# Moving small steps between the scans of a fused state-space and expert kernel, and one more pair of C products a chunk onto VectorE

## The reference

```
xn = LN(x)
B_t = xn @ W_B.T ; C_t = xn @ W_C.T                  # 16 numbers a row each
dt  = softplus((xn @ W_dt1.T) @ W_dt2.T + b_dt2)     # 256 a row
A   = -exp(log_A)                                    # 256 x 16
h   = exp(dt*A) * h + ((exp(dt*A) - 1)/A) * xn * B_t # for each of 256 x 16, along time
y   = sum over the 16 of h * C_t ; x1 = x + y + D_skip * xn
x2  = x1 + expert(LN(x1))                            # the expert of 8 with the largest logit,
                                                     # gelu(v @ W1 + b1) @ W2 + b2, 1024 hidden
```

## Time and profile before

| | |
|---|---|
| runs | 818.1 us median of 3 (811.09, 818.1, 821.95) |
| profiled execution | 813.52 us, of it 811.5 us span |
| busy in the span | TensorE 705.9 (87%), VectorE 526.8 (65%), ScalarE 480.7 (59%), GpSimd 513.6 (63%) |
| scans | from 34.0 to 489.2 us, eight chunks of 54.3 to 64.4 us |
| experts and end | from there to 811.5 us |

### The profile page before, as it was taken

The page is one execution under the profiler, slowest core; times in us unless marked ns, Lnnn a source line. Parts: engine busy times, 40 slices in busy tenths (PEclk is TensorE's granted clock), DMA queues, the critical chain, the costliest instruction groups (busy, mean ns, idle before and its releaser), DMA issues. The chain is left out here.

```text
span 811.5 us, 17757 instructions
## 1 busy us (share of the span) xinstructions
PE 705.9 (87%) x5882; PEld 614.9 (76%) x5883; DVE 526.8 (65%) x903; ACT 480.7 (59%) x983; POOL 513.6 (63%) x643
## 2 busy tenths in 40 slices
PE   7589798798898997986996877969999999999993
PEld 6467687677676776875776766759999999999992
DVE  4769988889988889888789986344333343333430
ACT  3388888888898997878875765313223332233320
POOL 1499987888879877989987775533333433334320
PEclk9579989899999998998987898789999999999997
DMA  9766853342343343464535459331111111111000
GB/s 211 178 215 215 276 175 94 103 133 67 108 141 105 90 122 98 85 108 102 96 92 57 110 174 310 47 41 46 57 44 59 36 42 48 47 54 46 29 8 1
DMA packets 45768, 82.61 MB, mean 102 GB/s; under 512 B 7800, under 2 KB 16253, under 8 KB 45696
## 3 DMA queue, kind: packets, MB, share of 16 engines
q1 hardware_dynamic: 39680, 69.08, 32.0%
q0 software_dynamic: 6016, 12.61, 6.0%
HBM read 70.50 MB, written 13.91 MB: 104 GB/s over the span
## 5 line engine op out<-in xcount | busy, mean ns | idle before, releaser
L628 POOL TENSOR_TENSOR w_sb<-w_sb,Csb 128x512 f32<-128x512 f32 x218 | 275.0, 1274 | 60.8 <-DVE w_sb L1178 42.6
L1178 DVE TENSOR_TENSOR_SCAN w_sb<-WW,hlast,w_sb 128x512 f32<-128x512 f32 x164 | 201.3, 1267 | 15.0 <-PE WW L994 12.0
L858 ACT ACTIVATE dt<-WW,b1c 128x128 f32<-128x128 f32 x312 | 89.2, 368 | 201.4 <-PE WW L1076 201.4
L979 PEld LDWEIGHTS WW<-b_sb,xin 64*128 64x128 f32 x2048 | 136.3, 202 | 73.4 <-issue 35.1
L979 PE MATMUL WW<-b_sb,xin 64*128 64x130 f32 (+1 forms) x2048 | 162.0, 301 | 34.3 <-DVE w_sb L1178 22.1
L794 ACT ACTIVATE w_sb<-dt,negA 128x512 f32<-128x512 f32 x256 | 170.0, 709 | 16.6 <-DVE dt L1207 9.5
L1012 PE MATMUL YY<-sm,w_sb 128*128 128x128 f32 x1024 | 147.8, 293 | 0.0
L1092 PE MATMUL misc<-w_sb,dt 128*128 x624 | 146.2, 389 | 1.4 <-issue 1.4
L688 POOL DMA_INDIRECT y_out<-CbX,ocol x39 | 44.4, 1140 | 149.1 <-DVE CbX L1492 148.4
L1092 PEld LDWEIGHTS misc<-w_sb,dt 128*128 128x128 f32 x624 | 119.1, 196 | 17.9 <-issue 2.3
L1012 PEld LDWEIGHTS YY<-sm,w_sb 128*128 128x128 f32 x1024 | 132.0, 161 | 0.2 <-POOL w_sb L628 0.2
(11 more groups left out here) (222 smaller groups left out, 789.1 us busy)
## 6 DMA issues: line engine op xcount, KB each, us to landing
w_sb<-c_rows SPq DMA_DIRECT2D x86, 256.0 KB, 4.0
CbX<-c_rows SPq DMA_DIRECT2D x42, 256.0 KB, 3.9
w_sb<-w_in SPq DMA_DIRECT2D x20, 512.0 KB, 6.4
token_rows<-row SPq DMA_DIRECT2D x16, 512.0 KB, 6.1
w_sb<-w_in SPq DMA_DIRECT2D x24, 256.0 KB, 5.1
xin<-x_in SPq DMA_DIRECT2D x16, 256.0 KB, 4.3
w_sb<-x_in SPq DMA_DIRECT2D x14, 256.0 KB, 9.2
b_sb<-b_in SPq DMA_DIRECT2D x1, 780.0 KB, 6.3
```

The costliest lines, as they stand in the source:

```text
L628: eng.tensor_tensor(by_time(hc[g % NHC]), in_tiles(hb_of(g)), in_tiles(Csb[i % NCS][:, :]), ALU.mult).then_inc(s_hcp, 1)
L858: g = eng.activation(hT[u % 2][:, j * P:(j + 1) * P], hps[u % 2][:, j * P:(j + 1) * P], ACT.Gelu, bias=b1c[u][:, j:j + 1])
L979: return eng.matmul(to[:, at:at + width], x_rows[rows, k, h * P:(h + 1) * P], band[rows, k, at % P:at % P + width], start=(k == 0), stop=( ...
L1178: eng.tensor_tensor_scan(hb_of(g) if pooled(g) else w_of(g), w_of(g), A[g % NA], hlast[(q - 1) % 2][:, h * N + n:h * N + n + 1] if q % NC ...
```

## The change

Four moves, nothing else. The work of every step stays as it is.

- `VECTOR_UNITS`: chunks 1 to 6 have the vector units 5, 8, 12 instead of 5, 10.
- xn0 goes from slot 2 to slot 3 of TensorE, ahead of xn1; the order of hops on each bank stays.
- `finish_rows` after scans 5 and 6 instead of 3 and 4; `ln2_stats` after 7 and 8 instead of 5 and 6; `aggregate` after 9 instead of 7.
- `dt_add` after scans 20 and 27 instead of 19 and 25; the first `u_times_x` after scan 30 instead of 29 (not in the last chunk); `first_table`, whose first step needs that, starts after scan 30 too and does two steps at its end.

```diff
-VECTOR_UNITS = [(4, 7, 11)] + [(5, 10)] * 6 + [(1, 5, 9, 13)]
+VECTOR_UNITS = [(4, 7, 11)] + [(5, 8, 12)] * 6 + [(1, 5, 9, 13)]
...
-        at = {1: [("cbt", q)], 2: [("xn0", q + 1)], 3: [("xn1", q + 1)], 4: [("bcd_a", q + 1)], 5: [("bcd", q + 1)],
+        at = {1: [("cbt", q)], 3: [("xn0", q + 1), ("xn1", q + 1)], 4: [("bcd_a", q + 1)], 5: [("bcd", q + 1)],
...
-                        if (j, gap) in ((3, 1), (4, 1)):
-                            finish_rows(q - 1, j - 3)
                         if (j, gap) in ((5, 1), (6, 1)):
-                            ln2_stats(j - 5, q - 1)
-                        if (j, gap) == (7, 1):
+                            finish_rows(q - 1, j - 5)
+                        if (j, gap) in ((7, 1), (8, 1)):
+                            ln2_stats(j - 7, q - 1)
+                        if (j, gap) == (9, 1):
                             aggregate(1, q - 1)
...
-                    if not last and (j, gap) in ((19, 1), (25, 1)):
-                        dt_add(q + 1, int(j == 25))
-                    if (j, gap) in (((9, 1), (11, 1)) if last else ((29, 1), (31, 0))):
+                    if not last and (j, gap) in ((20, 0), (27, 0)):
+                        dt_add(q + 1, int(j == 27))
+                    if (j, gap) in (((9, 1), (11, 1)) if last else ((30, 0), (31, 0))):
                         u_times_x(q, int(j in (11, 31)))
...
-                    if q == NQ - 2 and (j > 29 or (j, gap) == (29, 1)):
-                        first_table(2 * j + gap - 59)
+                    if q == NQ - 2 and j > 29:
+                        first_table(2 * j + gap - 60)
+                        if (j, gap) == (31, 1):
+                            first_table(4)
```

## The result

The changed kernel takes 792.54 us (median of 4 runs, 789.43 to 798.22) against 819.15 us before on the same chips (811.09 to 821.95): a ratio of 0.970, 95% interval 0.961 to 0.979. 791 was predicted, and 779 to 807 as the range. The execution that was profiled is the longest of the four, 798.22 us with a span of 796.4; its single chunks show where time went, its total understates the gain.

A forecast was written before the change was run, and what follows sets the result against it. VectorE's scan queue was taken as the longest chain, its idle time as the gain: 30.8 us over the chunks, less 4 for slips at ties, gives 27, so 791 us from the 818.1 median; range 779 to 807.

The forecast's parts named there:

- dt_add and u: VectorE, middle chunks: later dt_add and u_times_x cover waits of 2.49 and 0.58 us (dt_add) and 0.82 (u).
- the walk: Step-by-step timing of chunk 3 after the change, all engines: 50.15 us instead of 54.27, −4.1 us.
- A microsecond of its idle time is a microsecond of the chunk: VectorE's fixed-order scans are the longest chain, so its idle, 6.3 us in chunk 3, lengthens the chunk.
- xn0: TensorE, slot 2: moving xn0 to slot 3 removes the 3.43 us wait in chunk 3; scan 10 at 15.1, not 16.4.
- The units: Middle chunks, net one unit: VectorE +1.6 us, GpSimd −2 x 1.27 and a keep of h, ScalarE −2 x 0.71.
- finish_rows: TensorE, slot 2: y transposes newly wait for both finish_rows, 1.4 us in chunk 3, from 8.65 to 10.0.
- so I take full speed: TensorE, slot 2: new waits of 0.6 and 1.4 us, with a w between, would not lower the clock.
- scans 28 and 29 end 46.2: 0.5 us spare: Chunk 3: w of unit 15, behind u_a's wait for dt_add, is ready at 45.65, before scans 28 and 29 end.
- Rival A: TensorE's clock still falls in slot 2, making scan 10 0.9 us late: gain 21, 797 us; chance 0.15.
- Rival B: ScalarE sets the pace, scans wait for exponentials instead of w: 2.3 us a chunk, 14 in all, 804; chance 0.17.
- C: Waits only move, in TensorE's slots 2 to 4, and VectorE pays: 10 us added, 828 us; chance 0.08.
- The prediction's own list of signs: Chunks 1 to 4 at 50 to 52 us, dt_add waits under 6, no xn0 wait above 2, chunk 6 under 60, others.

## Why the prediction was right, and where not

- **dt_add and u: right, and the main gain.** Between the scans 20.8 us to none (the 22.2 of the prediction has 1.4 from ahead of the first scan), and 8.3 to 5.7, of which 3.0 is one wait in the last chunk. In the walk both the later dt_add and ScalarE's lighter slot 8 were needed for it. The runs show that either is enough, or nearly so (0.969 without the units, 0.973 without the later dt_add, beside 0.970).
- **"A microsecond of its idle time is a microsecond of the chunk": bookkeeping, and no proof that VectorE is the limit.** Over the scans its idle time went from 65.9 to 37.7 us and its work rose by 8.1, which makes the 20.1. But without the units it had 9 us less work in six chunks, and the scans took 434.9 us instead of 435.1: the work that went came back as idle time.
- **xn0: the wait right, what it brings only in part.** The 25.1 us are gone, and without this part the kernel loses the most, 5 us of scans. The walk had scan 10 start at 15.1 instead of 16.4. It starts at 15.70 in chunk 3; in chunk 1 it went from 18.14 to 15.46, in chunk 2 from 18.04 to 17.64, and in chunk 4 from 16.49 to 16.77.
- **The units: the cost right, the worth not seen.** 1.6 us of VectorE's work a chunk was right (busy 47.99 to 49.45 in chunk 3). In the set they give nothing outside chunks 5 and 6; alone they are worth 12 us.
- **finish_rows: the new wait right in place**, but it is a term that was sized too small: 1.4 a chunk in the walk, 1.9 in the mean and 3.31 at most. The walk let scan 6 start when the exponential of the trace before was ready, at 8.05. In the changed kernel ScalarE waits for x in chunks 2, 3, 4 and 6, scan 6 starts at 9.88 in chunk 2 and at 8.50 in chunk 3, and the second finish_rows, now behind it, passes every bit of this on to TensorE. That x is late was in the walk for chunk 2 alone, with 1.0 us of ScalarE's wait; it was 2.20.
- **Chunk by chunk.** The prediction's gains before its allowance for slips put chunk 1 at 50.65 (50.48 measured), chunk 0 at 51.75 (52.06), chunk 6 at 59.5 (59.60). Chunk 2 was to take 51.9 and took 53.18, chunk 3 50.15 and took 52.77, chunk 4 51.0 and took 54.61, chunk 5 53.3 and took 54.40, chunk 7 56.1 and took 58.03.
- **The step that failed is "so I take full speed"** together with "scans 28 and 29 end 46.2: 0.5 us spare". Rival A was right about the clock in slots 2 to 4, in five of its seven chunks (2 to 6). Its sum, a gain of 21, is also nearer to the 20.1 us that the profiled scans gained than the forecast's 27. It had only one of the two places. The other is slot 13 of chunk 3, where u_a's wait of 1.01 us for dt_add is followed by a w of 2.03 us; the walk had w of unit 15 ready at 45.65, it was at 47.85. Of these 2.2 us 0.9 are VectorE's, which came later to dt_add, and the rest TensorE's. Slot 13 cost 1.6 us in that one chunk. That the waits for x and finish_rows set the clock of slots 2 and 3 isn't shown: in the run with the second dt_add at scan 25 waits of 1.55 (chunk 3) and 2.65 us (chunk 4) for the rows were followed by full speed, in the changed kernel one of 1.92 was not. The rule of the Trainium skill that was weighed there ("TensorE: Matmul & The Clock Gate", Part 1, What's actually happening: the throttled state is the default, activity lifts it) pointed the right way: the two waits of slot 2 with little work between were followed by the lower clock in chunk 3. By itself it doesn't tell chunk 3 from chunk 1, which had the same order of waits and work and stayed at full speed.
- **Rival B (ScalarE sets the pace, 804): its time didn't come, its sign did in part.** Scans do wait for exponentials, 14.5 us by the two kinds of rows above instead of 6.7. They lie mostly in chunks 0, 6 and 7; in chunks 1 to 3 it is scan 6, with 0.21, 1.97 and 0.58 us. C's sign, a wait for w of over 1 us at scan 10, came in chunk 4 (1.38).
- **The prediction's own list of signs is met by half.** Right: no wait at xn0, dt_add under 6, 100 half products, chunk 6 under 60, the new wait. Not so: chunks 2 to 4 at 50 to 52 us, and products at 1.16 in slots 2 to 5.
- **The total was right in part by luck.** 30.8 by the walk, 4 off for ties that were named: 27, all of it in the scans; 26.6 is the difference of the medians. But for the profiled execution the prediction had 786.5, and it took 798.22: the scans gained 20.1 and not 27, and the rest took 5.0 longer. The execution profiled before was a short one (813.52 beside a median of 819.15), so some 6 us of the measured gain stand in no trace. The slips were real, but they were of the clock and of late x, more than of semaphore hops.

The changed kernel is not shown to be the best of its family: with the second dt_add after scan 25 it is at 0.963, the same with four units in chunk 6 at 0.965.

## What to carry to other kernels

When four engines are each near 90% busy, write the longest queue out and count the waits in front of its steps; moving a step one place later in that queue costs little where the next place's inputs are ready. Then count all idle time of the queue again, not only the wait that was cured: here 20.8 us went in front of dt_add and new waits for exponentials took the place of most of what w gave. Two edits that cure the same wait don't add up, so test the whole without each part as well as each part alone. After each move look at both sides: who waits for the moved step, and what it now stands behind. finish_rows, two scans later, stood behind scan 6 and handed that scan's wait on to TensorE; dt_add made a hop of TensorE wait 1 us, which was nearly hidden. And when one run's chunks look better, see at which scan the gain is there: it is hardly the edit's if it comes ahead of the moved step.

## What the runs showed of the hardware

A wait of 1.01 us of TensorE in slot 13 of chunk 3, where it had run without a longer one for over 30 us, was followed by sixteen products at 2.03 us and then 1.16 again. The same wait of 1.01 us in slot 13 of chunks 1, 2, 5 and 6 of the same execution was followed by 1.16. In other kernels waits of 2.65 us (second dt_add at scan 25, chunk 4) and 2.80 us (without the late rows, chunk 1) were followed by full speed. The length of the last wait alone doesn't say here whether the clock falls. What the lower clock cost in one place is seen from scan 28 to the end of chunk 3, with the same work and the same wait: 8.23 us with it and 6.63 without (the changed kernel, and the one without the late rows).

GpSimd's product took 1275 ns in the mean beside the added VectorE products and 1274 before them. These read one operand from PSUM, and the means show no slowdown of either engine (0.471 us a half product, 0.470 before).
